# Who builds the one-hots of a graph layer's edge loops: VectorE in one comparison, or POOL in four parts behind its gathers

## The chip, the cores and the metric

One core of one Trainium2 chip. The metric is the device time of one execution in microseconds. Engines: TensorE (PE; its weight loads are PEld), VectorE (DVE), ScalarE (ACT), GpSimd (POOL) and SyncE (SP), which only issues DMAs here.

## The reference

Two graph layers on 6250 nodes of 128 features, with 106250 edges that are sorted by their destination (`dst`). In short:

```python
h = relu(layernorm(x))
# layer 0: attention per feature over the edges that end in a node
a  = (h @ Ws.T + bs)[src] + (h @ Wd.T + bd)[dst]
e  = where(a >= 0, a, 0.2 * a)
sa = exp(e - segment_max(e, dst)[dst]); sa = sa / segment_sum(sa, dst)[dst]
x  = x + segment_sum((h @ Wv.T + bv)[src] * sa, dst)
h  = relu(layernorm(x))
# layer 1: two small networks per edge
s     = silu(silu(ea32 @ fc1 + b1) @ fc2 + b2) @ fc3 + b3
msg   = silu(h[src] @ W_node * s + ea16 @ W_sh)
al    = silu(silu([h[src,:64], h[dst,:64], ea32] @ aW1 + ab1) @ aW2 + ab2) @ aW3 + ab3
alpha = softmax(al, axis=edges).mean(heads)
x = x + layernorm(h + segment_sum(msg * alpha, dst) @ W_out)
```

Everything is float32; the tables that the one-hots multiply are split into three bf16 parts that together hold the float32 value.

## The kernel before

The edges are cut into 256 items of 512 edges (`NI`, `IT`), each with one block of 128 destination nodes. An index pass first finds each item's edge offset and node block; `mine_bc[:, i]` holds, per partition p, the code of node p of item i's block. Per layer, a node pass writes tables of rows to DRAM (`rows_d`: 256 float32 per node, read by source; `dst_d`: 3 x 128 bf16 per node, read by destination block). Then an edge loop goes over the 256 items, with everything of an item in tiles of 128 partitions by 512 edges.

The **one-hot** of an item is a 128 x 512 bf16 tile, `oht`: element (p, e) is 1 where edge e ends in node p of the block. TensorE multiplies the destination rows by it, so that each edge gets its destination's features. It is made by comparing the codes of the 512 edges, present on all partitions, with the code of node p (`mine_bc[:, i]`, one value per partition). `oht` is a ring of R = 4 tiles.

Each engine runs its own program, 32 laps of U = 8 items unrolled (POOL: 16 laps of 16), and engines meet at semaphores. `item(lap, u, d)` is the item d ahead of the step. One step does:

- **First loop, `layer0_edges` (L585).** SP (L642, L643) loads the edges' marks, spread to all partitions, and the block's destination rows, up to 8 items ahead. POOL copies the indices of 8 items from the big table into a small tile (L659) and issues four indirect DMAs per item (L662), each for 128 edges, 4 items ahead, into `G` (8 buffers); it waits until `wv_ready` says that item i-8's buffer is read. ACT: exp (L768), copy of the sum out of PSUM (L758), weights (L793), the turned one-hot (L779), `rest_of` (L782), and for item +4 the codes as absolute value into `who_t`, 2 buffers (L749). PE: `front` for item +2 (L686 transposes of the gathered rows, L689 the destination rows times the one-hot), `turn` for item 0 (L705, L712), `collect` for item -1 (L727, L730). DVE: `leaky` +1 (L829), `scale` -2 (L894), `running` +1 (scan, L840), `add` -2 (L905), `back` +1 (scan, L851), `weigh` 0 (L878), `gap` +1 (L864, L866), and last `onehot` for item +3 (L820). That comparison waits for `who_ready` and for the three readers of the ring's tile of item i-4: `a_ready` (front), `oh_ready` (turn), `rest_ready` (L782).
- **Second loop, `layer1_edges` (L920).** SP issues six loads per item (L1026 to L1030): codes, destination rows, and the edge attributes, which need no ScalarE pass. POOL gathers four times per item, 4 ahead (L1059), as above (index copy L1048), with one more hold in front of each gather: on `msg_ready`, `h1s`, `a1s` and `h2s` of earlier items. PE: `first` +3 (L1079 to L1094, with the one-hot in L1090), attributes (L1131, L1132), turn (L1145), and the later layers of both networks (L1105, L1109, L1120). ACT: the silus (L1198, L1208, L1216) and the store of the message (L1223). DVE: `onehot` for item +4 first (L1267; it waits for the item's loads `ld` and for `a1p` of item i-4), then the message (L1289, L1292), heads, and the scale's bias (L1277).

`hold(eng, passed, (sem, n))` (L72) is a wait followed by an increment of a bookkeeping semaphore. The pieces that the steps of the text speak of:

```python
# VectorE, first loop, L815 to L821
dve.wait_ge(who_ready, i + 1)
if after(i, R):
    dve.wait_ge(a_ready, i - R + 1)
    dve.wait_ge(oh_ready, i - R + 1)
    dve.wait_ge(rest_ready, i - R + 1)
nc.vector.tensor_scalar(oht[:, g, :], who_t[:, s % 2, :], mine_bc[:, bass.ds(i, 1)], None,
                        ALU.is_equal).then_inc(oht_ready, 1)
```

After the loops: the second loop's messages, kept in DRAM, are summed per block (`layer1_aggregate`), and `finish` multiplies, normalises and writes; its copies L1521 are the only POOL instructions of 128x128 elements that the text speaks of.

Of the kernel before, what the change touches and what calls it, by code (L numbers as in the profile page):

```python
# [13 lines left out]
F32 = mybir.dt.float32  # L14
# [78 lines left out]
def build(nc, x, src_pad, dst_pad, ea32, ea16, w0cat, b0cat, w1cat, fc1, b1, fc2, b2, fc3, b3, w_sh,  # L93
          aw1e, ab1, aw2, ab2, aw3, ab3, w_out, out):
    top = ExitStack()
    with top:
# [488 lines left out]
        def layer0_edges():  # L585

            st = ExitStack()
            with st:
                sidx = sb("l0_sidx", [P, 2, U * TJ], I32, st)
                G = sb("l0_G", [P, U, TJ, 2 * C], F32, st)  # L590
# [38 lines left out]
                with nc.Block() as block:  # L629
# [20 lines left out]
                    def _(pool):  # L650
                        def gather(lap, u, d):
# [6 lines left out]
                            if s == 0:  # L658
                                nc.gpsimd.tensor_copy(sidx[:, half, :], idx_tab[:, bass.ds(i * TJ, U * TJ)]).then_inc(idx_here, 1)  # L659
                                hold(pool, pool_passed, (idx_here, 2 * lp + half + 1))  # L660
                            for j in range(TJ):
                                nc.gpsimd.indirect_dma_start(  # L662
                                    out=G[:, s, j, :], out_offset=None, in_=rows_d[0][:, :],
                                    in_offset=bass.IndirectOffsetOnAxis(ap=sidx[:, half, s * TJ + j:s * TJ + j + 1], axis=0)).then_inc(gat[s], 16)

                        def step(lap, u):
                            gather(lap, u, 4)
# [3 lines left out]
                    def _(pe):  # L671
                        def front(lap, u, d):
# [7 lines left out]
                            pe.wait_ge(oht_ready, i + 1)  # L680
# [60 lines left out]
                    def _(act):  # L741
                        def whose(lap, u, d):
# [4 lines left out]
                            if after(i, 2):  # L747
                                act.wait_ge(oht_ready, i - 1)
# [55 lines left out]
                    def _(dve):  # L804
# [3 lines left out]

                        def onehot(lap, u, d):

                            i, s, lp = item(lap, u, d)
                            if not exists(i, NI):
                                return
                            g, gl = ring(s, lp)
                            dve.wait_ge(who_ready, i + 1)  # L815
                            if after(i, R):
                                dve.wait_ge(a_ready, i - R + 1)
                                dve.wait_ge(oh_ready, i - R + 1)
                                dve.wait_ge(rest_ready, i - R + 1)
                            nc.vector.tensor_scalar(oht[:, g, :], who_t[:, s % 2, :], mine_bc[:, bass.ds(i, 1)], None,  # L820
                                                    ALU.is_equal).then_inc(oht_ready, 1)  # L821
# [86 lines left out]
                        def step(lap, u):  # L908
# [7 lines left out]
                            onehot(lap, u, 3)  # L916
# [686 lines left out]
```

## Time and profile before

| what | value |
|---|---|
| runs | 4763.96, 4765.45, 4783.84 us; median 4765.45 |
| profiled execution | 4772.5 us, its span 4770.6 us |
| busy over the span | PE 67%, DVE 62%, POOL 46%, PEld 42%, ACT 36% |
| first edge loop | about 408 to 2160 us |
| second edge loop | about 2364 to 4180 us |

The rows name line, engine, operation and tiles. "Idle" is the time for which the engine stood still just before the instructions of a group, and behind the arrow what it waited for; "issue" means nothing that the profile shows. Time in which POOL gets a DMA ready between two gathers counts as idle.

### The profile page before, as it was taken

Reading aid. Unit: us, or ns where it says so; the run is one execution under the profiler, and the core shown is the slowest. Engines: PE = TensorE matmul, PEld = TensorE weight load, DVE = VectorE, ACT = ScalarE, POOL = GpSimd, SP = SyncE. Lnnn points to the kernel's source line nnn. Section 1 sums busy time; section 2 is a strip of 40 time slices with the busy share of each in tenths; the row PEclk is TensorE's granted clock in tenths of the full one; section 3 lists DMA queues with packets and bytes.
Section 4 is the critical chain, followed back from the end, with each engine's and each line's share of the span. In section 5 each row is a group of like instructions: output and inputs, shape, how many; then the busy total and the mean of one; then the engine's idle time right before and its main releaser. Section 6 shows DMA issues by size and latency. Waiting matters only on the chain. (4 is left out here: it accounts for less than half of the span.)

```text
span 4770.6 us, 78804 instructions
## 1 busy us (share of the span) xinstructions
PE 3193.8 (67%) x16644; PEld 2002.4 (42%) x16868; DVE 2941.9 (62%) x5753; ACT 1708.5 (36%) x3040; POOL 2200.2 (46%) x2274
## 2 busy tenths in 40 slices
PE   0024666666666666661489999999999999836664
PEld 0012444545455454540144444444444444435553
DVE  6576877778777877889733333333333333477776
ACT  0411444444444444440144444444444444410001
POOL 0004666666666766750155555555555555400001
PEclk9567888888888888885899999999999999979997
DMA  1934343334333433430355555666656566524552
GB/s 57 332 136 123 113 113 112 106 112 114 110 111 110 118 110 114 118 91 2 109 167 177 173 177 176 175 173 177 176 176 176 175 175 175 155 79 147 146 147 63
DMA packets 440626, 655.46 MB, mean 137 GB/s; under 512 B 81381, under 2 KB 294943, under 8 KB 440578
## 3 DMA queue, kind: packets, MB, share of 16 engines
q1 hardware_dynamic: 305410, 319.26, 23.3%
q0 software_dynamic: 98304, 268.57, 19.3%
q10 hardware_dynamic: 36864, 67.13, 3.7%
q8 instruction: 14, 0.23, 0.0%
q14 instruction: 34, 0.28, 0.0%
HBM read 530.01 MB, written 124.50 MB: 137 GB/s over the span
## 5 line engine op out<-in xcount | busy, mean ns | idle before, releaser
L662 POOL DMA_INDIRECT l_G<-rows_d,l_sidx x1024 | 1163.6, 1136 | 523.4 <-issue 299.9
L1059 POOL DMA_INDIRECT l_G<-rows_d,l_sidx x1024 | 972.2, 949 | 799.1 <-ACT l_h L1198 319.8
L686 PE MATMUL l_A<-ident,l_G 128*128 128x128 f32 x1024 | 196.6, 323 | 612.9 <-DVE l_oht L820 457.1
L1267 DVE TENSOR_SCALAR l_oht<-l_lo,mine_bc 128x512 bf16<-128x512 bf16 x256 | 95.9, 375 | 792.2 <-DMA l_sh<-sh_d 713.3
L1198 ACT ACTIVATE l_h<-l_H,l_cols 128x512 f32<-128x512 f32 x512 | 349.2, 682 | 487.3 <-remote 280.3
L730 PE MATMUL l_accp<-l_we,l_ohe 128*128 128x256 f32 x2048 | 521.6, 401 | 0.0
L1397 PE MATMUL ag_accp<-ag_msg,ag_pick 128*128 128x128 f32 x2048 | 303.6, 294 | 215.3 <-DVE ag_pick L1441 210.6
L686 PEld LDWEIGHTS l_A<-ident,l_G 128*128 128x128 f32 x1024 | 127.1, 160 | 712.3 <-issue 424.8
L730 PEld LDWEIGHTS l_accp<-l_we,l_ohe 128*128 128x128 f32 x2048 | 402.6, 208 | 49.8
L1397 PEld LDWEIGHTS ag_accp<-ag_msg,ag_pick 128*128 128x128 f32 x2048 | 256.7, 197 | 262.4 <-DVE ag_pick L1441 160.1
L758 ACT ACTIVATE l_e<-l_A 128x512 f32<-128x512 f32 x256 | 153.0, 597 | 586.4 <-remote 354.8
L878 DVE TENSOR_TENSOR l_we<-l_we,l_G 128x512 f32<-128x512 f32 x256 | 175.5, 685 | 271.5 <-issue 220.8
L840 DVE TENSOR_TENSOR_SCAN l_q<-l_lo,l_q,l_e 128x512 f32<-128x512 bf16 x256 | 326.3, 1275 | 0.4
L851 DVE TENSOR_TENSOR_SCAN l_top<-l_lo,l_q 128x512 f32<-128x512 bf16 x256 | 311.6, 1217 | 0.1
L1289 DVE TENSOR_TENSOR l_msg<-l_G,l_ST 128x512 f32<-128x512 f32 x256 | 174.7, 683 | 209.2 <-remote 128.9
L513 POOL COPY n_h_b<-H 128x128 f32 (+1 forms) x100 | 29.4, 297 | 579.7 <-DVE n_stats L556 445.3
L1441 DVE TENSOR_SCALAR ag_pick<-iota_row,local,ag_alpha 128x128 f32<-128x128 f32 x1024 | 285.4, 343 | 15.8 <-issue 12.9
L1105 PE MATMUL l_H<-l_h,big 128*128 128x512 f32 x512 | 269.8, 609 | 0.0
L1120 PE MATMUL l_SC<-l_h,big 128*128 128x512 f32 x512 | 268.9, 607 | 0.1
L1109 PE MATMUL l_A<-l_a,big 128*128 128x512 f32 x512 | 267.2, 604 | 0.0
L1216 ACT ACTIVATE l_msg<-l_msg 128x512 f32<-128x512 f32 x256 | 160.8, 628 | 259.0 <-DVE l_msg L1292 129.1
L492 PE MATMUL n_tp<-ident,n_h_b 128*128 128x128 f32 x100 | 28.1, 285 | 322.6 <-POOL n_h_b L513 322.6
(187 smaller groups left out, 6416.6 us busy)
## 6 DMA issues: line engine op xcount, KB each, us to landing
msg_d<-l_msg ACTq DMA_DIRECT2D x256, 256.0 KB
ag_msg<-msg_d SPq DMA_DIRECT2D x256, 256.0 KB, 2.6
l_G<-rows_d,l_sidx POOLq DMA_INDIRECT x2048
l_lo<-mark_d SPq DMA_DIRECT2D x256, 128.0 KB
l_lo<-code_d SPq DMA_DIRECT2D x256, 128.0 KB
l_fd<-dst_d SPq DMA_DIRECT2D x256, 96.0 KB
l_pd<-dst_d SPq DMA_DIRECT2D x256, 96.0 KB
l_ea<-ea_d SPq DMA_DIRECT2D x256, 96.0 KB
```

Source lines behind the costliest of these rows:

```text
L662: nc.gpsimd.indirect_dma_start(out=G[:, s, j, :], out_offset=None, in_=rows_d[0][:, :], in_offset=bass.IndirectOffsetOnAxis(ap=sidx[:, hal ...
L686: nc.tensor.matmul(av[:, j, :], G[:, s, j, 0:C], ident[:, :], is_transpose=True, start=(j == 0), stop=False, skip_group_check=True)
L730: last = nc.tensor.matmul(accp[b][:, 0:2 * C], oh_e[:, b, j, :], we_t[:, b, j, :], start=(j == 0), stop=(j == TJ - 1), skip_group_check=True)
L840: nc.vector.tensor_tensor_scan(q_t[:, b, :], lo_t[:, s, 0:IT], e_t[:, b, :], q_t[:, 1 - b, IT - 1:IT], ALU.min, ALU.max).then_inc(q_ready, 1)
L851: nc.vector.tensor_tensor_scan(top_t[:, b, ::-1], lo_t[:, s, IT:0:-1], q_t[:, b, ::-1], FAR, ALU.min, ALU.max).then_inc(top_ready, 1)
L1059: nc.gpsimd.indirect_dma_start(out=G[:, s, j, :], out_offset=None, in_=rows_d[1][:, :], in_offset=bass.IndirectOffsetOnAxis(ap=sidx[:, hal ...
L1105: nc.tensor.matmul(H2[:, :], w_fc2[:, :], h1_t[:, b, :], start=True, stop=True).then_inc(h2p, 1)
L1109: nc.tensor.matmul(A2[:, :], w_aw2[:, :], a1_t[:, b, :], start=True, stop=True).then_inc(a2p, 1)
L1120: nc.tensor.matmul(SC[:, :], w_fc3[:, :], h2_t[:, b, :], start=True, stop=True).then_inc(scp, 1)
L1198: nc.scalar.activation(out_t[:, s % 2, :], in_p[:, :], ACT.Silu, bias=cols[:, col:col + 1]).then_inc(ready, 1)
L1397: last = nc.tensor.matmul(accp[b][:, :], pick[:, b, j, :], msg_t[:, g, j, :], start=(j == 0), stop=(j == TJ - 1))
L1441: nc.vector.tensor_scalar(pick[:, b, j, :], iota_row[:, :], local[:, bass.ds(i * TJ + j, 1)], al[:, bass.ds(i * TJ + j, 1)], ALU.is_equal, ...
```

## The change

POOL makes the one-hot of both loops. Behind each of its four gathers it compares one quarter (128 of the 512 edges) and writes that quarter of `oht`. `oht_ready` goes up by 4 per item, so every waiter multiplies by `TJ` = 4. VectorE's two `onehot` functions go. The node codes of 8 items are copied into a small tile `mine_t` beside the indices. In the first loop the gathers run 4 items ahead as before, the parts 3 ahead; in the second loop both are of the same item, and the four extra holds before its gathers are gone. The waits that VectorE's comparison had are now POOL's, at part 0.

```diff
 # layer0_edges, @block.gpsimd
                             if s == 0:
                                 nc.gpsimd.tensor_copy(sidx[:, half, :], idx_tab[:, bass.ds(i * TJ, U * TJ)]).then_inc(idx_here, 1)
-                                hold(pool, pool_passed, (idx_here, 2 * lp + half + 1))
+                                nc.gpsimd.tensor_copy(mine_t[:, half, :], mine_bc[:, bass.ds(i, U)]).then_inc(idx_here, 1)
+                                hold(pool, pool_passed, (idx_here, 2 * (2 * lp + half + 1)))
...
+                        def onehot(lap, u, d, j):
...
+                            g, part = v % R, slice(j * P, (j + 1) * P)
+                            if j == 0:
+                                hold(pool, pool_passed, (who_ready, i + 1))
+                                if after(i, R):
+                                    hold(pool, pool_passed,
+                                         (a_ready, i - R + 1),
+                                         (oh_ready, i - R + 1),
+                                         (rest_ready, i - R + 1))
+                            nc.gpsimd.tensor_scalar(oht[:, g, part], who_t[:, v % 2, part], mine_t[:, v // U, v % U:v % U + 1], None,
+                                                    ALU.is_equal).then_inc(oht_ready, 1)
+
+                        def step(lap, u):
+                            ready(lap, u, 4)
                             for j in range(TJ):
+                                rows(lap, u, 4, j)
+                                onehot(lap, u, 3, j)
...
 # layer0_edges, PE front; ACT whose
-                            pe.wait_ge(oht_ready, i + 1)
+                            pe.wait_ge(oht_ready, TJ * (i + 1))
...
-                                act.wait_ge(oht_ready, i - 1)
+                                act.wait_ge(oht_ready, TJ * (i - 1))
...
 # layer0_edges, VectorE step
-                            onehot(lap, u, 3)
...
 # layer1_edges, @block.gpsimd
+                        def onehot(i, v, lp, j):
+
+                            s, half, g, part = v % U, v // U, v % R, slice(j * P, (j + 1) * P)
+                            if j == 0:
+                                hold(pool, pool_passed, (ld[s], 96 * (2 * lp + half + 1)))
+                                if after(i, R):
+                                    hold(pool, pool_passed, (a1p, i - R + 1))
+                            nc.gpsimd.tensor_scalar(oht[:, g, part], lo_t[:, s, part], mine_t[:, half, s:s + 1], None,
+                                                    ALU.is_equal).then_inc(oht_ready, 1)
...
                             for j in range(TJ):
-                                if j == 0 and after(i, 6):
-                                    hold(pool, pool_passed, (msg_ready, i - 5))
-                                if j == 1 and after(i, 2):
-                                    hold(pool, pool_passed, (h1s, i - 1))
-                                if j == 2 and after(i, 2):
-                                    hold(pool, pool_passed, (a1s, i - 1))
-                                if j == 3 and after(i, 3):
-                                    hold(pool, pool_passed, (h2s, i - 2))
                                 nc.gpsimd.indirect_dma_start(
                                     out=G[:, s, j, :], out_offset=None, in_=rows_d[1][:, :],
                                     in_offset=bass.IndirectOffsetOnAxis(ap=sidx[:, half, s * TJ + j:s * TJ + j + 1], axis=0)).then_inc(gat[s], 16)
+                                onehot(i, v, lp, j)
...
 # layer1_edges, VectorE step
-                            onehot(lap, u, 4)
                             message(lap, u, 0)
```

## Rows read from the trace of the kernel before

**Rows 1.** Stretches: busy us (and instructions) of each engine in the edge loops.

```profile
408.00:2160.00 1752.00, 1123.61 (x6034) 854.64 (x6131) 1368.69 (x2303) 748.42 (x1536) 1174.85 (x1056) 0.86 0.39 110
...
2364.00:4180.00 1816.00, 1616.47 (x8064) 812.38 (x8192) 680.78 (x1173) 821.47 (x1282) 978.98 (x1055) 0.97 0.59 172
```

**Rows 2.** Groups, VectorE, first loop: busy us, mean ns | idle before, releaser.

```profile
L840 DVE TENSOR_TENSOR_SCAN l_q<-l_lo,l_q,l_e 128x512 f32<-128x512 bf16 x256 | 326.3, 1275 | 0.4
L851 DVE TENSOR_TENSOR_SCAN l_top<-l_lo,l_q 128x512 f32<-128x512 bf16 x256 | 311.6, 1217 | 0.1
L878 DVE TENSOR_TENSOR l_we<-l_we,l_G 128x512 f32<-128x512 f32 x256 | 175.5, 685 | 271.5 <-issue 220.8 <-ACT l_we L793 49.2
L829 DVE SCALAR_TENSOR_TENSOR l_e<-l_e 128x512 f32<-128x512 f32 x256 | 175.3, 685 | 9.0 <-ACT l_e L758 6.1 <-issue 2.9
L866 DVE TENSOR_TENSOR l_w<-l_e,l_top 128x512 f32<-128x512 f32 x256 | 174.5, 682 | 0.0
L820 DVE TENSOR_SCALAR l_oht<-l_who,mine_bc 128x512 bf16<-128x512 bf16 x256 | 89.1, 348 | 0.0
```

**Rows 3.** Timeline, first loop: start us, us, what, and idle before it.

```profile
1409.56 1.27 DVE L840 TENSOR_TENSOR_SCAN l_q<-l_lo,l_q,l_e 128x512 f32<-128x512 bf16 x1
1414.76 1.28 DVE L840 TENSOR_TENSOR_SCAN l_q<-l_lo,l_q,l_e 128x512 f32<-128x512 bf16 x1
...
1416.26 1.22 DVE L851 TENSOR_TENSOR_SCAN l_top<-l_lo,l_q 128x512 f32<-128x512 bf16 x1
1421.82 0.69 DVE L878 TENSOR_TENSOR l_we<-l_we,l_G 128x512 f32<-128x512 f32 x1 [4.33 <-issue]
...
1404.32 1.82 POOL L662 DMA_INDIRECT l_G<-rows_d,l_sidx  x1 [0.30 <-issue]
```

**Rows 4.** Groups; line view (ns min/median/max; first, last start): first loop's gathers.

```profile
L662 POOL DMA_INDIRECT l_G<-rows_d,l_sidx x1024 | 1163.6, 1136 | 523.4 <-issue 299.9 <-DVE l_we L878 203.9 <-POOL l_sidx L659 19.6
...
L662 POOL DMA_INDIRECT l_G<-rows_d,l_sidx x1024: 945/1052/1937, 409.4 to 2124.8; - x171
```

**Rows 5.** The same two views of the second loop's gathers.

```profile
L1059 POOL DMA_INDIRECT l_G<-rows_d,l_sidx x1024 | 972.2, 949 | 799.1 <-ACT l_h L1198 319.8 <-issue 313.2 <-DVE l_msg L1289 80.9
...
L1059 POOL DMA_INDIRECT l_G<-rows_d,l_sidx x1024: 942/949/1056, 2364.7 to 4141.1; - x171
```

**Rows 6.** Groups: VectorE's comparison of the second loop.

```profile
L1267 DVE TENSOR_SCALAR l_oht<-l_lo,mine_bc 128x512 bf16<-128x512 bf16 x256 | 95.9, 375 | 792.2 <-DMA l_sh<-sh_d 713.3 <-issue 78.6
```

**Rows 7.** Waits of SyncE's queue: us in total, times, longest us.

```profile
SPq L77 <- DVE l_top L851: 513.5, 153, 7.8
...
SPq L77 <- PE l_SHP L1132: 0.7, 1, 0.7
```

**Rows 8.** Groups: TensorE's first instruction of front.

```profile
L686 PE MATMUL l_A<-ident,l_G 128*128 128x128 f32 x1024 | 196.6, 323 | 612.9 <-DVE l_oht L820 457.1 <-issue 154.9
```

**Rows 9.** Groups: POOL's 128x128 copies at the kernel's end.

```profile
L1521 POOL COPY fi_ab<-big 128x128 f32 (+1 forms) x50 | 14.7, 296 | 488.4 <-POOLq L1356 470.8 <-PE fi_tp L1503 17.6
```

**Rows 10.** Groups; line view of L659: POOL's small copies in both loops.

```profile
L659 POOL COPY l_sidx<-idx_tab 128x32 int32 (+1 forms) x32 | 11.2, 351 | 32.4 <-DVE l_we L878 19.6 <-POOLq L459 12.6
...
L1048 POOL COPY l_sidx<-idx_tab 128x32 int32 (+1 forms) x32 | 7.0, 220 | 12.7 <-POOLq L459 12.5
...
L659 POOL COPY l_sidx<-idx_tab x32: 212/230/839, 408.2 to 2071.2; 128x32 int32 x28, 128x32 int32<-128x32 int32 x4
```

**Rows 11.** Timeline of POOL, second loop.

```profile
3204.55 0.95 POOL L1059 DMA_INDIRECT l_G<-rows_d,l_sidx  x1 [0.31 <-issue]
3205.51 0.22 POOL L1048 COPY l_sidx<-idx_tab 128x32 int32 x1
3206.63 0.97 POOL L1059 DMA_INDIRECT l_G<-rows_d,l_sidx  x1 [0.90 <-POOL l_sidx L1048]
```

**Rows 12.** Timeline, first loop: a copy of POOL that meets L866.

```profile
727.03 0.68 DVE L866 TENSOR_TENSOR l_w<-l_e,l_top 128x512 f32<-128x512 f32 x1
727.24 0.54 POOL L659 COPY l_sidx<-idx_tab 128x32 int32 x1 [0.80 <-DVE l_we L878]
```

More of the change, by code:

```diff
@@ L650, in _, with ready @@
                     def _(pool):
-                        def gather(lap, u, d):
+                        def ready(lap, u, d):
                             i, v, lp = item(lap, u, d, 2 * U)
@@ L666, in step, with rows @@
-                        def step(lap, u):
-                            gather(lap, u, 4)
+                                nc.gpsimd.tensor_copy(mine_t[:, half, :], mine_bc[:, bass.ds(i, U)]).then_inc(idx_here, 1)
+                                hold(pool, pool_passed, (idx_here, 2 * (2 * lp + half + 1)))
+                        def rows(lap, u, d, j):
+                            i, v, lp = item(lap, u, d, 2 * U)
+                            s, half = v % U, v // U
+                            if not exists(i, NI):
+                                return
+                            nc.gpsimd.indirect_dma_start(
+                                out=G[:, s, j, :], out_offset=None, in_=rows_d[0][:, :],
+                                in_offset=bass.IndirectOffsetOnAxis(ap=sidx[:, half, s * TJ + j:s * TJ + j + 1], axis=0)).then_inc(gat[s], 16)
@@ new lines, in onehot @@
+                        def onehot(lap, u, d, j):
+                            i, v, lp = item(lap, u, d, 2 * U)
+                            if not exists(i, NI):
+                                return
+                            g, part = v % R, slice(j * P, (j + 1) * P)
[8 more added lines that the diff above has]
+                                                    ALU.is_equal).then_inc(oht_ready, 1)
@@ L807, in _ @@
                         dve.wait_ge(zeroed, 3)
[L809 to L821, printed above, removed]
                         def leaky(lap, u, d):
@@ L1048, in step @@
                                 nc.gpsimd.tensor_copy(sidx[:, half, :], idx_tab[:, bass.ds(i * TJ, U * TJ)]).then_inc(idx_here, 1)
[L1049 removed]
+                                nc.gpsimd.tensor_copy(mine_t[:, half, :], mine_bc[:, bass.ds(i, U)]).then_inc(idx_here, 1)
+                                hold(pool, pool_passed, (idx_here, 2 * (2 * lp + half + 1)))
                             for j in range(TJ):
[L1051 to L1058 removed]
                                 nc.gpsimd.indirect_dma_start(
```

18 lines of the change are left out of this document (3 added, 15 removed).

## The prediction

> **What bounds the kernel now.** I read the table of stretches first [rows 1]. The two edge loops take 1752 and 1816 us of the 4770.6 us span, and the change touches nothing outside them. In the first loop VectorE is busy 1369 of 1752 us (78%), the largest share. In the second it is TensorE, 1616 of 1816 us (89%), while VectorE has only 681. So the same edit meets two different machines.
>
> First loop. VectorE's 1369 us are 5.35 us per item, the two scans and three other 512-wide instructions foremost [rows 2], and in a smooth stretch one item takes 5.20 us from scan to scan (1409.56 to 1414.76 [rows 3]). POOL issues four gathers per item. The line of the gathers [rows 4] runs from 409.4 to 2124.8 us, 1715 us for 256 items, 6.70 us each. The gap between 5.2 and 6.7 is pauses: at 1417.48 VectorE finishes a scan and starts again at 1421.82 [rows 3]. I can't name their cause and carry them along. What matters is how full POOL is: a gather takes 1.136 us in the mean, and 0.30 us stand before it for no reason that the profile shows (299.9 us over 916 gaps), so 4 x (1.136 + 0.30) = 5.74 us of 6.70. POOL waits for VectorE 203.9 us in the whole loop. It is the second fullest resource, 86% taken, and nobody sees it in the busy column, because the gap isn't busy time.
>
> Second loop. Gathers take 0.949 us [rows 5], because nothing slows them; from 2364.7 to 4141.1 us they make 6.94 us per item, with 4 x (0.949 + 0.30) = 5.0 us of POOL in it. VectorE's comparison is the first thing in its step and waits 713.3 us for the item's loads [rows 6]. SyncE, which issues six loads per item, waits for a free buffer once for 0.7 us in this loop, against 513.5 us in the first [rows 7]: there it always has the next load to issue, and the loads set the pace together with TensorE.
>
> **Removed.** VectorE loses 256 x 0.348 = 89 us and 256 x 0.375 = 96 us [rows 2, 6]. In the first loop TensorE waits for this very comparison 457.1 us [rows 8], but it waits for it because it is the last instruction of a step that is full; what goes is the 0.35 us, at most 89 us. In the second loop VectorE has 62% idle: nothing. The four holds that spaced POOL's second-loop gathers out (319.8 us of waiting for ScalarE's L1198 [rows 5]) go too. They are slack and not work: POOL waits because it is ahead. Their cover is the 1.9 us per item in which POOL has nothing to do, and the change fills it.
>
> **Added, on POOL, per part:** a 128x128 comparison, bf16 in and out, behind each gather. No row shows one. The nearest by shape is POOL's 128x128 copy, 0.296 us [rows 9]. Its lower bound is the 128x32 copy at 0.22 us, the upper the longest small copy of the first loop, 0.839 us [rows 10]. In the second loop I take 0.30. In the first, VectorE is in the way: a copy that starts at 727.24 under L866 ends at 727.78, 0.07 us behind it [rows 12], and the gathers are 0.19 us longer than in the second loop. At a period of 7.7 us instead of 6.7 VectorE is less dense, and I take 0.16 for each, gather and part: 1.11 and 0.46. In front of a compute instruction that follows a gather there is no gap (3204.55 + 0.95, next start 3205.51 [rows 11]). In front of a gather that follows a compute instruction the only rows have 0.90 with a semaphore in between [rows 11]; between two gathers it is 0.30. Between part j and gather j+1 there is no semaphore, so I take 0.30, with 0 and 0.9 as the ends.
>
> **Sum of the first loop.** 1.11 + 0.30 + 0.01 + 0.46 = 1.88 us per part, 7.50 per item. Every eighth item has two small copies in place of one and a wait for them: 2 x 0.35 + 0.90 = 1.6 us [rows 10, 11], 0.20 per item (before, 0.16). That is 7.70 us per item on POOL, more than the 6.70 at which the loop runs with its pauses. POOL becomes the bound: 256 x (7.70 - 6.70) = +256 us. VectorE's saved 0.35 us is then worth nothing. The extra semaphores are not: the part j = 0 waits for the ring of four one-hots (front, turn and rest of item i-4) and for ScalarE's copy of the codes, and the next gather of item i+1 is queued behind it. From POOL's last part of an item to the rest_ready that POOL needs two steps on there are a front, a turn and three ScalarE copies, which today all fit in a smooth step of 5.2 us [rows 3]; POOL asks for it 7.7 us and a gather later. So the ring leaves some 4 us, and only longer pauses reach POOL. ScalarE pays nothing: its wait for the codes' buffer looks two items back.
>
> **Sum of the second loop.** 0.949 + 0.30 + 0.01 + 0.30 = 1.56 per part, 6.24 per item, and (0.44 + 0.90) / 8 = 0.17: 6.41 us, under 6.94. But the first part of an item waits for the item's loads and holds up its gathers 1 to 3, which until now ran a step ahead of the loads. They end some 4 x 1.56 - 0.95 = 5.3 us behind the loads' landing plus their own transfer. SyncE never waits for a buffer, so this delay eats slack and not rate. For POOL at 92% of the pace, tied to loads that come unevenly, I add 0.1 us per item, 25 us. The moved reads cost no DMA: gathers and loads are the same ones, on the same queues.
>
> Together 4770.6 + 256 + 25 = 5052 us in the profiled execution's terms (it reads 4772.5 for a span of 4770.6). The median of the runs is 7 us lower, 4765.45: I forecast **5045 us**. What a measurement of this kernel can tell from no change is about 0.5%, 24 us.
>
> **Where row and rule differ.** A copy of POOL that meets a long VectorE instruction ends with it: 727.78 against 727.71 [rows 12]. Yet the mean of the 32 copies is only 0.13 us over the second loop's [rows 10], and that of the 1024 gathers 0.19; the sum rests on these means. If every part arrived at random and waited out whatever it met of L829, L840, L851, L878 and L866, it would lose half the sum of their squares over the period, 4.5 / 2 / 7.7 = 0.29 us [rows 2], 0.13 more than I take. The Trainium skill, SBUF — State Buffer, "Who interferes with whom", states just this: a VectorE instruction with two SBUF inputs and a GpSimd instruction that reads SBUF share a read port, and the later one blocks fully. By that rule it would be the second rival below, 5180 us.
>
> **Rivals.**
> - Faster, 4690: POOL keeps up. If gathers and parts find VectorE idle, the part is 0.949 + 0.30 + 0.01 + 0.296 = 1.555 us and the item 6.22 + 0.20 = 6.42, 0.28 under today's: 256 x 0.28 = 72 us faster, paid by the lighter VectorE. It decides from (6.70 - 0.20) / 4 = 1.62 us per part. For it: the first loop's gathers go down to 945 ns with a median of 1052 [rows 4], and its copies have a median of 230 [rows 10]. Against it: VectorE spends 4.54 us per item in the five long two-input instructions [rows 2] and they don't go away. Chance 0.14.
> - No change, 4765: the change does not do what it says, since the 0.30 before a gather vanishes behind a compute instruction and the part takes its place: 1.11 + 0.01 + 0.46 = 1.58, and 6.3 + 0.2 = 6.5 us, under 6.70, with the ring's waits on top about equal. Chance 0.09.
> - The port blocks fully, 5180: 0.29 us in place of 0.16 behind each part is 4 x 0.13 x 256 = 133 us more. For it: [rows 12]. Against it: the means [rows 4, 10], and that VectorE stands still for part of each item once POOL is the bound. Chance 0.12.
> - Much slower, 5250 to 5600: the comparison on POOL is dear, or port and gap are. At 0.60 us for a part the first loop has 4 x (1.11 + 0.31 + 0.60) + 0.20 = 8.3 us (+410), the second 4 x 1.86 + 0.17 = 7.6 (+170): 5350. Also here: POOL, held at the loads, becomes the second loop's chain. The loads of item i are issued at i-8 and the gathers' end lies 5 steps on; if SyncE's slack is smaller than I read, 5.3 + 2 us over 5 steps is 1.46 us per item, +374. Chance 0.23.
> - The forecast itself, 4900 to 5130: chance 0.42.
>
> **Numbers.** Slower by over 0.5%: 0.42 + 0.12 + 0.23 = 0.77. Within 0.5%: 0.09. Faster: 0.14. The range leaves out most of the faster case and the far end of the dear one: 4760 to 5400. The likeliest case alone is 4900 to 5130.
>
> **What would show it.** In the first loop POOL's gathers and parts back to back with the 0.30 gap and hardly any wait for L878; VectorE's share down from 78% to about 62%; TensorE's granted clock lower than 0.86 there. In the second loop nearly the old length, POOL's first part waiting for the loads and TensorE waiting for gathers where it waited for little. It is wrong if POOL's parts take under 0.25 us with no gap before gathers (faster or equal), if the second loop grows by more than 60 us (the tie to the loads costs rate), or if VectorE's own instructions lengthen by more than a few ns, which would mean that POOL's reads stop VectorE and not the other way.

## The result, and the profile of the changed kernel

The changed kernel takes **5638.47 us** (5638.41 to 5640.57), beside 4771.26 us for the kernel before in the same comparison: a ratio of **1.182 [1.179, 1.184]**, slower by 867 us. The prediction said 5045 us, with 4760 to 5400 as its range. The side was right, the size was not: the time lies beyond the range's upper end. The profiled execution has a span of 5636.0 us against 4770.6, 865.4 us more.

The two stretches that answer to [rows 1], busy us of PE, PEld, VectorE, ScalarE and POOL, then TensorE's granted clock, DMA share and GB/s:

```profile
408.00:2840.00 2432.00, 1327.46 (x6048) 993.42 (x6144) 1354.07 (x2079) 751.18 (x1538) 2173.31 (x2112) 0.80 0.28 80
3034.00:5010.00 1976.00, 1643.45 (x7986) 825.94 (x8115) 600.21 (x900) 832.12 (x1272) 1713.29 (x2112) 0.95 0.53 157
```

POOL is now the fullest engine of both: 2173 of 2432 us (89%) and 1713 of 1976 us (87%), against 67% and 54% before. The line views of the two gathers (duration in ns as least, median and most, then first and last start) give the lengths that stand against [rows 4, 5]:

```profile
L669 POOL DMA_INDIRECT l_G<-rows_d,l_sidx x1024: 945/1036/1894, 409.4 to 2811.6; - x171
...
L1074 POOL DMA_INDIRECT l_G<-rows_d,l_sidx x1024: 1015/1033/1047, 3035.5 to 5005.6; - x171
```

The first loop went from 1715 to 2402 us (+687), the second from 1776 to 1970 (+194). That is 881 us; the stretch between the loops is 16 us shorter, and 865 remain. Per item (1023 intervals are 255.75 items): 9.39 us for 6.71, and 7.70 for 6.95. The groups show what an item is made of (busy us, mean ns | idle before, and what released it):

```profile
L669 POOL DMA_INDIRECT l_G<-rows_d,l_sidx x1024 | 1240.5, 1211 | 200.8 <-issue 174.3
L1074 POOL DMA_INDIRECT l_G<-rows_d,l_sidx x1024 | 1058.3, 1034 | 200.2 <-issue 167.8
L686 POOL TENSOR_SCALAR l_oht<-l_who,l_mine 128x128 bf16<-128x128 bf16 x1024 | 900.2, 879 | 35.4
L712 PE MATMUL l_A<-ident,l_G 128*128 128x128 f32 x1024 | 250.3, 390 | 1086.4 <-POOL l_oht L686 1086.4
...
L1057 POOL TENSOR_SCALAR l_oht<-l_lo,l_mine 128x128 bf16<-128x128 bf16 x1024 | 645.8, 631 | 59.5 <-DMA l_sh<-sh_d 24.3
...
L1103 PE MATMUL l_A<-ident,l_G 128*128 128x128 f32 x1024 | 164.0, 284 | 305.7 <-DMA l_G<-rows_d,l_sidx 252.7
```

To be seen here: a comparison of 128 columns takes **0.879 us** in the first loop and **0.631 us** in the second, where the prediction put 0.46 and 0.30. POOL waits for hardly anybody: 35.4 us before 1024 comparisons are the 0.035 us between two instructions, and the only wait of the second loop for loads is one of 24.3 us. Summed over its gaps, POOL waits for other engines and for loads 7 us in the first loop (223 before) and 31 us in the second (481 before). TensorE waits for the one-hot, 1086.4 us where it was 457.1 [rows 8]. The steady picture of POOL in the second loop (start us, us, what, idle before):

```profile
4000.08 0.63 POOL L1057 TENSOR_SCALAR l_oht<-l_lo,l_mine 128x128 bf16<-128x128 bf16 x1
4000.88 1.03 POOL L1074 DMA_INDIRECT l_G<-rows_d,l_sidx  x1 [0.17 <-issue]
4001.95 0.63 POOL L1057 TENSOR_SCALAR l_oht<-l_lo,l_mine 128x128 bf16<-128x128 bf16 x1
```

A part with its gather is 1.034 + 0.035 + 0.631 + 0.17 = 1.87 us, times four 7.48, and 7.70 with the small copies and the waits. In the first loop the same sum is 1.211 + 0.035 + 0.879 + 0.17 = 2.30, times four 9.18, and 9.39 with the copies. There, parts and gathers stretch where VectorE has a long instruction; the part below begins under L878, the gather under the scan L852:

```profile
1403.72 1.04 POOL L669 DMA_INDIRECT l_G<-rows_d,l_sidx  x1 [0.17 <-issue]
1404.78 1.51 POOL L686 TENSOR_SCALAR l_oht<-l_who,l_mine 128x128 bf16<-128x128 bf16 x1
1406.46 1.86 POOL L669 DMA_INDIRECT l_G<-rows_d,l_sidx  x1 [0.17 <-issue]
...
1404.55 0.74 DVE L878 TENSOR_TENSOR l_w<-l_e,l_top 128x512 f32<-128x512 f32 x1
1406.21 1.27 DVE L852 TENSOR_TENSOR_SCAN l_q<-l_lo,l_q,l_e 128x512 f32<-128x512 bf16 x1
```

SyncE, which in the second loop had always a load to issue [rows 7], now waits for buffers in both:

```profile
SPq L77 <- DVE l_top L863: 1462.3, 248, 7.7
SPq L77 <- PE l_SHP L1148: 531.1, 180, 6.1
```

So POOL's own program sets the pace of both loops, and the other engines wait behind it.

### The profile page after: what moved, and what is told of

Same layout as the page of the kernel before. It is cut to its first block and busy times, and to the rows that moved or that the text cites. A ratio compares the mean times of both kernels' runs of the same rounds, so it can differ in the third digit from the quotient of the medians.

```text
span 5636.0 us, 79975 instructions
## 1 busy us (share of the span) xinstructions
PE 3437.6 (61%) x16644; PEld 2162.2 (38%) x16868; DVE 2862.0 (51%) x5241; ACT 1727.3 (31%) x3040; POOL 3932.9 (70%) x4386
## 5 line engine op out<-in xcount | busy, mean ns | idle before, releaser
L669 POOL DMA_INDIRECT l_G<-rows_d,l_sidx x1024 | 1240.5, 1211 | 200.8 <-issue 174.3
L1074 POOL DMA_INDIRECT l_G<-rows_d,l_sidx x1024 | 1058.3, 1034 | 200.2 <-issue 167.8
L686 POOL TENSOR_SCALAR l_oht<-l_who,l_mine 128x128 bf16<-128x128 bf16 x1024 | 900.2, 879 | 35.4
L712 PE MATMUL l_A<-ident,l_G 128*128 128x128 f32 x1024 | 250.3, 390 | 1086.4 <-POOL l_oht L686 1086.4
L1057 POOL TENSOR_SCALAR l_oht<-l_lo,l_mine 128x128 bf16<-128x128 bf16 x1024 | 645.8, 631 | 59.5 <-DMA l_sh<-sh_d 24.3
L712 PEld LDWEIGHTS l_A<-ident,l_G 128*128 128x128 f32 x1024 | 160.9, 194 | 1189.1 <-POOL l_oht L686 784.1
L756 PE MATMUL l_accp<-l_we,l_ohe 128*128 128x256 f32 x2048 | 549.1, 417 | 0.0
L756 PEld LDWEIGHTS l_accp<-l_we,l_ohe 128*128 128x128 f32 x2048 | 425.5, 220 | 57.9
L1103 PE MATMUL l_A<-ident,l_G 128*128 128x128 f32 x1024 | 164.0, 284 | 305.7 <-DMA l_G<-rows_d,l_sidx 252.7
L1214 ACT ACTIVATE l_a<-l_A,l_cols 128x512 f32<-128x512 f32 x256 | 176.1, 688 | 560.8 <-PE l_A L1110 477.6
L1282 DVE TENSOR_SCALAR big<-l_SC,l_cols 128x512 f32<-128x512 f32 x256 | 192.2, 751 | 306.6 <-PE l_SC L1136 241.0
L852 DVE TENSOR_TENSOR_SCAN l_q<-l_lo,l_q,l_e 128x512 f32<-128x512 bf16 x256 | 325.9, 1273 | 0.3
L715 PE MATMUL l_A<-l_oht,l_fd 128*128 128x512 bf16 x672 | 297.5, 564 | 5.9 <-issue 5.5
```

The lines of the kernel that those rows point to most:

```text
L669: nc.gpsimd.indirect_dma_start(out=G[:, s, j, :], out_offset=None, in_=rows_d[0][:, :], in_offset=bass.IndirectOffsetOnAxis(ap=sidx[:, hal ...
L686: nc.gpsimd.tensor_scalar(oht[:, g, part], who_t[:, v % 2, part], mine_t[:, v // U, v % U:v % U + 1], None, ALU.is_equal).then_inc(oht_rea ...
L712: nc.tensor.matmul(av[:, j, :], G[:, s, j, 0:C], ident[:, :], is_transpose=True, start=(j == 0), stop=False, skip_group_check=True)
L715: last = nc.tensor.matmul(A[b][:, :], fd_t[:, s, k * C:(k + 1) * C], oht[:, g, :], start=False, stop=(k == 2), skip_group_check=True)
L756: last = nc.tensor.matmul(accp[b][:, 0:2 * C], oh_e[:, b, j, :], we_t[:, b, j, :], start=(j == 0), stop=(j == TJ - 1), skip_group_check=True)
L852: nc.vector.tensor_tensor_scan(q_t[:, b, :], lo_t[:, s, 0:IT], e_t[:, b, :], q_t[:, 1 - b, IT - 1:IT], ALU.min, ALU.max).then_inc(q_ready, 1)
```

## The experiments

The theory after the result: POOL's own occupancy is the whole of it, and the one-hot's place in the chain costs nothing. The rivals: the chain (TensorE waits for parts that come late), and a tie of POOL to the loads. Times are compared with runs of the kernel before on the same chip. These had 4771 to 4778 us in all comparisons but two: once 4216, once 4720. `first_only`, `second_only`, `pool_load`, `forms_a`, `forms_b` and `one_512` were timed once each; what they are read for is far above the spread of the kernel before, 4767 to 4786 us in fourteen executions.

**One loop at a time.** `first_only` has the first half of the diff, `second_only` the second half.

> Occupancy (my theory after the result): each loop is paced by POOL's own sequence of gather, gap, part, gap, and the two loops do not touch each other. The first loop of the changed kernel took 687 us more from first to last gather (2402 against 1715), the second 194 (1970 against 1776). So with the first loop alone changed: 4771 + 687 = about 5450 us, POOL's item at 9.4 us there and the second loop at 6.95 as before. Rival: the loops share something (the slower first loop leaves TensorE at a lower clock or DMA queues in another state) and the second loop moves too, by over 30 us.

> Occupancy: 4771 + 194 = about 4965 us, 7.7 us per item in the second loop, gathers at 1.034 us and parts at 0.631 us with POOL back to back. Rival (the tie to the loads, which I had feared in the prediction): POOL's first part of an item waits for the item's loads and the parts' rate is not what counts; then POOL shows waits in front of part 0 that add up to 100 us or more.

`first_only` took 5436.7 us beside 4774.6 (+662), `second_only` 4970.5 (+196). Together they make 858 of 867 us: to within 9 us the loops don't meddle with each other. In `first_only` the gather took 1206 and the part 883 ns, in `second_only` 1033 and 630. POOL's wait for the loads in `second_only`:

```profile
POOL l_oht L1046 <- DMA l_sh<-sh_d: 23.8, 1, 23.8
```

Once, at the loop's start. Beyond it the tie to the loads costs nothing here.

**What is the relief of VectorE worth?**

```diff
-nc.vector.tensor_scalar(oht[:, g, :], who_t[:, s % 2, :], mine_bc[:, bass.ds(i, 1)], ...
+nc.vector.tensor_scalar(oht[:, g, 0:1 if after(i, R) else IT], who_t[:, s % 2, 0:1 if after(i, R) else IT], ...
```

> Leaves out: VectorE compares only one column of 512 from item 4 on, in both loops; the other columns keep old contents. It shows what taking the comparison off VectorE is worth when nobody pays for it. If VectorE's full step paces the first loop: 0.35 - 0.06 us less per item, 256 x 0.29 = 74 us, 4697 us. Rival: POOL at 5.74 us of 6.70 per item and the pauses already share the pace; then the gain is under 30 us. In the second loop both say nothing.

4720.3 us, ratio 0.989 [0.987, 0.990], 54 us less. In the traced execution, the fastest of its six (4694.2 us), the gathers of the first loop run from 409.4 to 2064.2 us, 1655 us for 1715, and the second loop has 1772 for 1776. But the edit takes less off VectorE than was expected. The comparison of one column still takes 0.211 us where that of 512 took 0.348, so 0.14 us went per item and not 0.29:

```profile
L820 DVE TENSOR_SCALAR l_oht<-l_who,mine_bc 128x1 bf16<-128x1 bf16 (+1 forms) x256 | 53.9, 211 | 0.0
```

So the run says that relief of VectorE is worth something in the first loop and nothing that shows in the second. What taking the whole comparison away would be worth, it does not show; with POOL as the bound, in the changed kernel, it is worth nothing.

**POOL's load without the chain.** The kernel before, VectorE making every one-hot, and behind each of POOL's gathers one more comparison of constants into a tile that nobody reads:

```diff
+nc.gpsimd.tensor_scalar(spare_b[:, :], ident_b[:, :], iota_col[:, 0:1], None, ALU.is_equal).then_inc(spared, 1)
```

> VectorE makes the one-hots as in the kernel before; POOL in addition does a 128x128 bf16 comparison of two constants into a spare tile behind each gather, that nobody waits for. Occupancy: the time is as in the changed kernel, 5600 to 5750 us, though no reader waits for a part (VectorE's comparison is back too, and the holds of the second loop are still there). Rival (chain): what costs is that TensorE, ScalarE and VectorE wait for the parts and POOL waits for the ring and the loads; then this kernel stays under 5300 us.

5607.8 us, within 31 us of the changed kernel, though no other engine waits for the added work. The two gather groups:

```profile
L676 POOL DMA_INDIRECT l_G<-rows_d,l_sidx x1024 | 1237.7, 1209 | 215.5 <-POOL l_spare_b L658 44.8 <-POOL l_spare_b L660 43.9 <-POOL l_spare_b L662 43.6
L1088 POOL DMA_INDIRECT l_G<-rows_d,l_sidx x1024 | 1059.4, 1035 | 223.8 <-POOL l_spare_b L1062 44.1 <-POOL l_spare_b L1064 43.6 <-POOL l_spare_b L1060 41.6
```

The same 1.21 and 1.035 us as in the changed kernel, and POOL waits for others 0 and 32 us in the two loops. This decides it: the chain's theory falls, POOL's occupancy stays.

**What in the comparison is dear?** As `pool_load`, but each of the four instructions of an item has its own form, in both loops.

```diff
+if j == 1: nc.gpsimd.tensor_scalar(spare_f[:, :], ident[:, :], iota_col[:, 0:1], None, ALU.is_equal).then_inc(spared, 1)
+if j == 2: nc.gpsimd.tensor_scalar(spare_b[:, :], ident_b[:, :], 1.0, None, ALU.is_equal).then_inc(spared, 1)
+if j == 3: nc.gpsimd.memset(spare_b[:, :], 0.0).then_inc(spared, 1)
...
+if j == 0: nc.gpsimd.tensor_copy(spare_b[:, :], ident_b[:, :]).then_inc(spared, 1)
+if j == 1: nc.gpsimd.tensor_scalar(spare_b[:, 0:32], ident_b[:, 0:32], iota_col[:, 0:1], None, ALU.is_equal).then_inc(spared, 1)
```

The first three lines are of `forms_a`, the last two of `forms_b`.

> The kernel before plus one extra POOL instruction on constants behind each gather, four forms of 128x128: j=0 comparison bf16 to bf16 with a per-partition scalar (0.63 us where VectorE is not in the way), j=1 the same in float32, j=2 bf16 with a constant scalar, j=3 a memset of bf16, which reads nothing. Theory 1 (a comparison costs POOL per element what a copy does not): the float32 one is as dear as the bf16 one, over 0.55 us in the second loop. Rival (bf16, or the scalar fetched per partition, is what is dear): the float32 form or the constant form is at 0.35 us or less. Port: in the first loop the memset, which reads nothing from SBUF, is as long as in the second (within 0.03 us) if only reads are blocked; if writes are blocked too it grows by 0.2 us like the others.

> As forms_a, with j=0 a copy bf16 to bf16 128x128, j=1 the comparison of 32 columns only, j=2 a comparison float32 to bf16, j=3 a float32 copy. Theory 1: the copies take 0.30 us, the 32-column comparison about 0.30 (0.19 fixed and 3.4 ns per column), so that the price is per column. Rival (a fixed price of the comparison's code): 32 columns take over 0.5 us. Rival (conversion of bf16): the bf16 copy takes 0.5 us or more against 0.30 for float32.

`forms_a` took 5260.8 us and `forms_b` 5069.1 us, beside 4771.8. Groups of `forms_a`; L658 to L664 are of the first loop, L1060 to L1066 of the second:

```profile
L658 POOL TENSOR_SCALAR l_spare_b<-ident_b,iota_col 128x128 bf16<-128x128 bf16 x256 | 219.1, 856 | 8.5
L1062 POOL TENSOR_SCALAR l_spare_f<-ident,iota_col 128x128 f32<-128x128 f32 x256 | 163.2, 637 | 8.7
L1060 POOL TENSOR_SCALAR l_spare_b<-ident_b,iota_col 128x128 bf16<-128x128 bf16 x256 | 161.9, 632 | 9.1
L1064 POOL TENSOR_SCALAR l_spare_b<-ident_b 128x128 bf16<-128x128 bf16 x256 | 143.9, 562 | 7.4
L1066 POOL MEMSET l_spare_b<- 128x128 bf16 x256 | 57.9, 226 | 0.2
L664 POOL MEMSET l_spare_b<- 128x128 bf16 x256 | 57.9, 226 | 0.2
```

And of `forms_b`:

```profile
L658 POOL COPY l_spare_b<-ident_b 128x128 bf16<-128x128 bf16 x256 | 110.9, 433 | 1.6
L1062 POOL TENSOR_SCALAR l_spare_b<-ident_b,iota_col 128x32 bf16<-128x32 bf16 x256 | 103.3, 403 | 9.1
L1060 POOL COPY l_spare_b<-ident_b 128x128 bf16<-128x128 bf16 x256 | 76.1, 297 | 1.5
L664 POOL COPY l_spare_f<-ident 128x128 f32<-128x128 f32 x256 | 141.5, 553 | 1.7
L1066 POOL COPY l_spare_f<-ident 128x128 f32<-128x128 f32 x256 | 77.4, 302 | 1.6
```

The type counts for next to nothing (632 and 637 ns for the comparison, 297 and 302 for the copy). The operation counts: at the same shape a copy takes 0.30 and the comparison 0.63 us. A comparison against a constant saves 70 ns of it. The comparison of 32 columns takes 0.403 us, between the 0.30 that a price per column would give by the expectation and the 0.5 of a fixed price. In the first loop all forms that read grow: the comparison by 0.22, the bf16 copy by 0.14, the float32 copy by 0.25 us. The memset, which reads nothing, stays at 226 ns in both loops. How much a form grows also depends on its place in the item (one and the same comparison has 771 to 956 ns at the four places of `pool_load`), so the three numbers don't rank the forms.

The traces also tell what a gather costs behind each form, in the second loops: 0.95 us behind another gather, with a gap of 0.305 before it (the kernel before); 0.96 behind a memset (`forms_a`), 0.98 behind a copy (`forms_b`) and 1.03 behind a comparison (both), with a gap of 0.17 each.

**One comparison of 512 columns** behind the four gathers, instead of four of 128:

```diff
-g, part = v % R, slice(j * P, (j + 1) * P)
+g, part = v % R, slice(0, IT)
...
-                                onehot(lap, u, 3, j)
+                            onehot(lap, u, 3, 0)
```

> The changed kernel with one 128x512 comparison behind the four gathers, instead of four 128x128 behind one each. If the price is per column (3.4 ns), it takes 0.19 + 512 x 0.0034 = 1.95 us, the item in the second loop 4 x (0.95 + 0.30) + 1.95 + 0.2 = 7.2 us against 7.70, and the kernel about 5636 - 0.5 x 512 = 5400 us. If the price is mostly fixed, it takes about 0.8 us, POOL needs 6.0 us per item in the second loop, under its old pace of 6.94, and the kernel comes to 5150 us or less.

5020.3 us, beside 4771.8: better than the change by 618 us, worse than the kernel before. Neither expectation holds. In the second loop the comparison takes 1.59 us, between 0.8 and 1.95, and the kernel is faster than both said because the first loop saves too (2402 to 2016 us; the second 1970 to 1738).

```profile
L669 POOL DMA_INDIRECT l_G<-rows_d,l_sidx x1024 | 1139.5, 1113 | 301.5 <-issue 275.2 <-POOL l_mine L661 26.3
L1075 POOL DMA_INDIRECT l_G<-rows_d,l_sidx x1024 | 994.6, 971 | 303.0 <-issue 275.3 <-POOL l_mine L1072 25.4 <-PE l_A L1111 1.5
L686 POOL TENSOR_SCALAR l_oht<-l_who,l_mine 128x512 bf16<-128x512 bf16 x256 | 556.4, 2174 | 8.4
L1058 POOL TENSOR_SCALAR l_oht<-l_lo,l_mine 128x512 bf16<-128x512 bf16 x256 | 406.3, 1587 | 29.0 <-DMA l_sh<-sh_d 20.6
```

With 32, 128 and 512 columns at 0.403, 0.631 and 1.587 us in second loops, the price is some 0.32 us for an instruction and 2.4 to 2.5 ns for a column ((1587 - 631) / 384 and (631 - 403) / 96). Cutting it in four therefore cost 4 x 0.631 - 1.587 = 0.94 us per item, 241 us over a loop. In the first loop the four parts are 3.52 us and the single one 2.17.

**The holds that went.** Only the four extra holds before the second loop's gathers are taken out of the kernel before.

```diff
-if j == 0 and after(i, 6):
-    hold(pool, pool_passed, (msg_ready, i - 5))
...
```

> The kernel before without the four holds that spread POOL's gathers in the second loop. The change removes them too. Theory: they are slack, the time stays within 0.5% (4750 to 4795 us). Rival: they keep the gathers' transfers out of the way of the loads, and without them the second loop grows by 30 us or more, which would be a part of the 194 us that the changed kernel loses there.

4895.1 us, ratio 1.025 [1.021, 1.029]: the theory that they are slack has fallen. Without them the second loop has 7.33 us per item for 6.95, some 99 us from first to last gather: in the kernel before they were worth 123 us in all. In the changed kernel POOL is full and they add nothing (`second_only` and `pool_load`, one without and one with holds, have the same 7.70 us).

**Is spacing what they do?** I took the pauses of [rows 3] for an effect of gathers that stand too close. `spaced_both` has a memset of 0.226 us behind every gather and no holds, `spaced_held` has it in the second loop alone and keeps the holds; VectorE makes the one-hots in both.

```diff
+nc.gpsimd.memset(spare[:, :], 0.0).then_inc(spared, 1)
```

> VectorE makes the one-hots as before; POOL does a memset of a spare 128x128 bf16 tile (0.226 us, reads nothing) behind each gather in both loops, and the second loop's four holds are gone. Theory (spacing): wherever something stands between two gathers, SyncE's stretches of 0.7 us per instruction vanish (810 such slots in the second loop of before, 832 without holds, 22 in the changed kernel) and with them the pauses; the second loop then runs at about 6.5 us per item instead of 6.95, 115 us less, against 7.3 without holds and filler. In the first loop POOL's item is 4 x (1.21 + 0.04 + 0.23 + 0.17) + 0.1 = 6.7 us, so nothing is won there. Together 4650 to 4670 us. Rival: the slow stretches go away in the changed kernel only because everything is slower there; then a filler does nothing and the second loop stays at the 7.3 us of the kernel without holds, about 4890 us.

> Filler memsets in the second loop alone, with its four holds kept. If spacing alone counts, the holds are now idle and the second loop is as in spaced_both, 6.5 us per item, 4655 us together. If the holds do something of their own (keep gathers from running ahead), this one is faster in the second loop than spaced_both by 30 us or more. If neither spacing nor holds are it, 4771 us.

Beside these two the kernel before took **4216 us**, not 4771. `spaced_both` had 4478.9 us, ratio 1.062 [1.060, 1.064], and `spaced_held` 4218.5, ratio 1.000 [0.999, 1.001]. The first loop of `spaced_held` is the old code without a change, and yet its gathers run in 1383 us, not 1715:

```profile
L662 POOL DMA_INDIRECT l_G<-rows_d,l_sidx x1024: 942/1001/1885, 409.0 to 1791.9; - x171
...
L662 POOL DMA_INDIRECT l_G<-rows_d,l_sidx x1024 | 1039.5, 1015 | 331.2 <-issue 304.9 <-POOL l_sidx L659 26.0 <-DVE l_we L878 0.3
```

Here POOL waits for VectorE 0.3 us in the whole loop, where it was 203.9 [rows 4]. Its gathers, its own gaps and its small copies fill the 1383 us: without the pauses POOL is the bound of the old first loop already. `spaced_both` shows it from the other side. Its memsets make that loop 1641 us, of which POOL waits for others 10 us, and these 258 us more are nearly all of the 263 that it loses.

So one and the same code runs under two conditions, and the next comparison, on the same chip, had the other one again.

> The kernel before, unchanged, for a trace beside the next three. On the chip of the last two runs it took 4216 us and not 4771, and its first loop, unchanged in spaced_held, ran at 5.4 us per item without pauses. So there are two conditions: with pauses (4771, SyncE slow in some 500 and 800 slots) and without (4216, hardly any). Either this run is near 4771 with those slots, or near 4216 without.

> The changed kernel. POOL's own sequence shows no pauses in its trace, so by the occupancy theory it takes the same in both conditions up to what single instructions differ (gathers of 0.95 behind a filler in place of 1.03 us): 5450 to 5640 us. Where the kernel before takes 4216, that is 1.29 to 1.34 of it; where it takes 4771, 1.18.

> As spaced_both. Where the kernel before takes 4771 us: spacing predicts 4650 to 4670 us and few slow slots, its rival about 4890. Where it takes 4216 there are no pauses to remove and it repeats 4479.

> As spaced_held. Where the kernel before takes 4771 us: 4655 us if spacing counts, 4771 if not. Where it takes 4216 it repeats 4218.

`before_again` 4775.2, `after_again` 5622.8 (ratio 1.177 [1.173, 1.182]), `spaced_both_again` 4852.4 (1.016 [1.012, 1.020]), `spaced_held_again` 4792.7 (1.004 [1.003, 1.005]). What differs is seen on SyncE's queue. Its timeline in `before_again` (start us, us, what):

```profile
3009.49 0.00 SPq L1026 DMA_DIRECT2D l_lo<-code_d  x1
3010.24 0.01 SPq L1027 DMA_DIRECT2D l_pd<-dst_d  x1
3010.97 0.02 SPq L1029 DMA_DIRECT2D l_ea<-ea_d  x1
...
3016.48 0.35 SPq L1026 DMA_DIRECT2D l_lo<-code_d  x1
3017.03 0.35 SPq L1027 DMA_DIRECT2D l_pd<-dst_d  x1
3017.49 0.36 SPq L1029 DMA_DIRECT2D l_ea<-ea_d  x1
```

From one issue to the next SyncE takes 0.46 us in smooth stretches and 0.73 in others. I counted slow steps in the middle 80% of the two loops: instructions of SyncE's sequencer that last 0.55 to 0.80 us or have a pause of that length behind them. There are 461 and 849 in `before_again`, 0 and 4 in `spaced_held`, 0 and 22 in the changed kernel. With the memset they didn't vanish (509 and 929 in `spaced_both_again`), and the time came near the rival's 4890, not to 4670. Yet a memset hardly spaces: it takes the place of a part of the gap, and from one gather's start to the next the median in the second loop is 1.34 us for 1.25 before.

These runs also tell when the holds are worth something. Where the kernel before takes 4771 to 4778 us, the second loop without them is longer, with a memset (1862 us for 1793) as without (1875 for 1776). Where it takes 4216, it is not (1553 for 1571).

**A wider spacing, and the changed kernel beside it.** `paced_second` has a comparison of 32 columns as the filler, in the second loop alone, holds kept.

```diff
+nc.gpsimd.tensor_scalar(spare[:, 0:32], ident_b[:, 0:32], iota_col[:, 0:1], None, ALU.is_equal).then_inc(spared, 1)
```

> The kernel before, with one more instruction of POOL behind each gather of the second loop: a comparison of 32 columns of constants into a spare tile, which nobody waits for (0.403 us in the second loop of forms_b). The holds stay. Where the kernel before takes near 4771 us, with its pauses: the pauses' theory says that a second loop whose gathers are spaced to some 1.6 us has few pauses, so the loop takes about 1700 us for 1776 and the kernel some 4700 us (ratio 0.985). The rival, that forms_b's second loop was short because its four different instructions or its slower first loop changed something else, gives 4765 to 4790 us (ratio 1.00). Where the kernel before has no pauses (near 4216 us), POOL has 4 x (1.03 + 0.18 + 0.40 + 0.03) = 6.6 us per item for 6.1, and the kernel is some 120 us slower (ratio 1.03).

> The changed kernel in one round, beside the kernel before on the same chip. If the kernel before has its pauses (near 4771 us), the ratio is 1.18. If it has none (near 4216 us), POOL's 9.4 and 7.7 us per item stay what they are, the changed kernel takes about 5620 us, and the ratio is 1.33; if it is itself faster there, POOL's prices depend on that condition too.

The kernel before had 4719.8 us here. `paced_second` took 4730.3, ratio 1.002 [0.999, 1.004]; `after_third` 5641.1, ratio 1.196 [1.192, 1.200]. The slow steps of SyncE's queue in the second loop fell to 61, but the loop still took 1758 us. The row of its gathers says why it could hardly take less:

```profile
L1061 POOL DMA_INDIRECT l_G<-rows_d,l_sidx x1024 | 1059.3, 1034 | 256.0 <-POOL l_spare L1066 159.7 <-issue 45.7 <-POOL l_sidx L1050 30.0
```

Gathers 1059 us, the gaps before them 256, comparisons and their gaps 441: POOL's own program fills the loop, and POOL waits for others only 20 us of the 1758. The expectation had 6.6 us per item for POOL, measured are 6.87. The same holds for `forms_b`, whose POOL waits for others 18 us of 1701. So whether fewer slow steps or wider spacing would shorten a loop that POOL doesn't fill is not shown by this run. No version that I ran beats the kernel before. (`relief` is faster, but doesn't make the one-hots.)

## Why the prediction was wrong

- **The price of a part, the step that failed.** The prediction took POOL's copy of the same shape, 0.296 us, as the nearest row and set 0.30 and 0.46. The comparison has 0.631 and 0.879. Against the sum that is 4 x 0.33 x 256 = 339 us in the second loop and 4 x 0.42 x 256 = 429 us in the first. The upper bound, 0.839 us, was the slowest of 32 small copies; it held for the second loop, and in the first the mean itself went beyond it. A price of 0.60 was in the fourth rival, but its 5350 us joined it to an untouched 1.11 us for the gather: that rival had the mechanism and was still too low.
- **The gap, sized too large.** 0.30 us was set before a gather; it is 0.17 behind a compute instruction, plus 0.035 before the part: 0.21 for 0.31. This gives back 4 x 0.10 x 256 = 102 us in each loop.
- **The gather, sized too small.** 1.211 for 1.11 in the first loop (+103 us), 1.034 for 0.949 in the second (+87 us). In the second loop the longer gather comes with the instruction before it: behind a comparison 1.03 us, behind a memset 0.96, nearly as behind another gather, and the gap before it is 0.13 shorter behind each. `one_512`, where only one gather in four stands behind one, has 971 ns, which is the mixture (3 x 949 + 1034) / 4 = 970.
- **The sums.** First loop: 7.70 + 4 x (0.42 - 0.10 + 0.10) = 9.38 us, measured 9.39. Second: 6.41 + 4 x (0.33 - 0.10 + 0.085) = 7.67, measured 7.70. That the misses of gap and gather cancel in the first loop (-102 and +103 us) is luck; the price of the part is what is left. That POOL becomes the bound in the first loop was right; in the second, POOL was taken to stay under 6.94, and that fell with the price.
- **Tie to the loads**, 25 us and up to 374 in a rival: one wait of 24.3 us at the loop's start, and nothing per item. The prediction's sign for it, a second loop longer by more than 60 us, did show (+194), but for another reason, POOL's own sum. The bound of the second loop turned over before the tie could matter.
- **"They are slack and not work"**, said of the holds: wrong for the kernel before at 4772 us, where they are worth 123 us (`no_holds`); in the changed kernel their absence costs nothing that shows. Why they are worth it is open.
- **VectorE's saved 0.35 us**: at most 89 us in the first loop, nothing in the second, and nothing once POOL is the bound. The last is what the changed kernel shows. Alone, and with only 0.14 us of it gone, it gave 54 us.
- **How the port is shared.** The prediction took 0.16 us per instruction from means and gave full blocking 0.29, as a rival of chance 0.12 (5180 us, the third in its list). Measured: +0.25 for the part (0.631 to 0.879), +0.18 for the gather (1.034 to 1.211). The rival's own formula with the real period gives 4.5 / 2 / 9.39 = 0.24 us, so its mechanism was nearer than the term of the sum. The Trainium skill, SBUF — State Buffer, "Who interferes with whom", states that a GpSimd instruction that reads SBUF shares a read port with VectorE's two-input instructions. The trace agrees: the copy and the comparison grow, the memset does not. It calls the shared ports an exclusive lock and says, of VectorE's two-port modes, that whoever issues first has them for the whole instruction; the last section shows where the measurement differs.
- **What showed as expected**: hardly a wait of POOL, VectorE's share down (56%, I had said 62), TensorE's granted clock down from 0.86 to 0.80 in the first loop.

## What to carry to other kernels

Before work moves to POOL, price it there by the operation, not by the shape: at 128 x 128 a memset took 0.226, a copy 0.297 and a comparison with a value per partition 0.631 us, and the comparison of 512 columns cost VectorE 0.35 to 0.38 us and POOL 1.59, or 2.52 in four parts. An engine whose busy share is 67% can be nearly full: count the gaps before its gathers (at 4216 us POOL filled the old first loop with a busy share of 76%), and ask of every part how many times its fixed price is paid. Put the suspected load alone into the kernel before, with nobody waiting for it: if the time is that of the change, the chain is innocent. Look at the row of what you put in or took out: a filler can fill the engine, and an instruction cut to one column is not gone.

## What the runs showed of the hardware that I had not expected

**The port is shared both ways.** The prediction held that VectorE's instructions would keep their length. The line view of VectorE's second scan in the changed kernel, of 1217 ns before [rows 2]:

```profile
L863 DVE TENSOR_TENSOR_SCAN l_top<-l_lo,l_q x256: 1208/1382/1393, 427.4 to 2827.1; 128x512 f32<-128x512 bf16 x128
```

Of the 256 scans, the 124 that begin while a part of POOL is under way take 1212 ns in the mean; these parts began under the scan before and take 1632 ns. The 130 that are already running when a part begins, some 0.65 us after their own start, take 1387. So here the earlier instruction isn't untouched: it loses 0.17 us to the later one, and a lock held to the end, as the Trainium skill's page has it, would cost it nothing. `pool_load` repeats it: 173 second scans into which a comparison falls 0.6 to 0.8 us after their start take 1381 ns. It is not always so. In the changed kernel 116 first scans (L852), in which a part begins within 0.1 us of their start, take 1272 ns, for 1275 before. What decides it is open. In `one_512` the 29 second scans in which the comparison began took 1701 ns, and the group of L879, the same operation as L866, had 920 ns for 682. With memsets as the filler (`spaced_both`) the scan kept its 1217 ns. That VectorE's instructions lengthen was one of the prediction's signs of being wrong; it showed, and POOL's instructions lengthened too.

**Two conditions for one program.** On one chip the kernel before took 4216 us in one comparison and 4778 in another, the same in every run of each; on a second chip it had 4720. The changed kernel took 5623 to 5641 us in three comparisons with 4720 to 4778 us before. It wasn't run in the 4216 us condition. If POOL's prices are the same there, the change would cost a third and not 18% (an estimate: 5623 / 4216 = 1.33). What makes the condition is open. TensorE's granted clock differs with it, 0.97 over the first loop of `spaced_held` and 0.85 in `before_again`; in the second loops it is 0.99 and 0.98 while the times are 1571 and 1772 us, so there the clock is not the cause. Putting work behind POOL's gathers didn't remove the pauses where it left POOL with time to spare (memsets, a pitch of 1.34 to 1.45 us). Where it filled POOL, as in the changed kernel, there are few slow steps or the loop is at POOL's own sum, so that a cure could not be told from a full engine. The second loop of `forms_b` took 1701 us for 1776, with more work on POOL: that is POOL's own sum, and why the loop can be shorter than that of the kernel before is open too.
